# Layer 2's attention of the first batch moved to the end of layer 1, its weights split early and kept in DRAM for both batches

## What is computed

```
# layer 1: 16 heads of 128, each token sees the blocks of 64 within two of its own
x = layernorm(x + softmax(q k^T / sqrt(128) + band_mask) v @ Wo)
# layer 2: a router scores each token; the 128 best of each batch are processed
scores = x @ w_router ;  idx = sort(top_k(scores, 128))
sel = x[b, idx]                       # 256 tokens in all
h = rms_norm(sel) ;  q, k, v = h @ wq + bq, h @ wk + bk, h @ wv + bv
q, k = rope(q, idx), rope(k, idx)     # 16 query heads, 8 key/value heads
x1 = sel + causal_softmax(q k^T / sqrt(128)) v @ wo    # over the 256 tokens
y  = x1 + silu(rms_norm(x1) @ w_gate) * (rms_norm(x1) @ w_up) @ w_down
x[b, idx] = sigmoid(scores) * y + (1 - sigmoid(scores)) * sel ;  x = layernorm(x)
```

## Time and profile before

| | us |
|---|---|
| median of 3 runs | 1465.58 (1464.21 to 1465.84) |
| the profiled execution | 1463.87 |
| its span, first to last instruction | 1462.0 |
| PE busy | 1292.3 (88%) |
| DVE, ACT, POOL busy | 947.5, 588.4, 99.2 |
| PE matmuls of layer 1's q, k, v projections and of the units (proj, L835) | 694.3 |

### The profile page before, as it was taken

The page is one execution under the profiler, slowest core; times in us unless marked ns, Lnnn a source line. Parts: engine busy times, 40 slices in busy tenths (PEclk is TensorE's granted clock), DMA queues, the critical chain, the costliest instruction groups (busy, mean ns, idle before and its releaser), DMA issues.

```text
span 1462.0 us, 20054 instructions
## 1 busy us (share of the span) xinstructions
PE 1292.3 (88%) x7624; PEld 1138.4 (78%) x7624; DVE 947.5 (65%) x2523; ACT 588.4 (40%) x1478; POOL 99.2 (7%) x139
## 2 busy tenths in 40 slices
PE   6999999999999999999998998999999995266696
PEld 5888888888888888787777887788887884265595
DVE  4556566666666666887866676666767667656464
ACT  4444444444444444334434444444444431023341
POOL 0000000000000000110000000000000001112272
PEclk9999999999999999999999999999999998598798
DMA  5000110101010120132112143353434236195251
GB/s 180 30 15 30 44 44 15 44 15 44 15 44 22 52 73 30 63 112 72 44 33 72 67 144 125 138 177 123 170 129 144 98 121 232 55 393 190 86 187 43
DMA packets 75967, 135.76 MB, mean 93 GB/s; under 512 B 4384, under 2 KB 51488, under 8 KB 69728
## 3 DMA queue, kind: packets, MB, share of 16 engines
q1 hardware_dynamic: 75456, 133.19, 26.5%
...
## 4 chain that ended last, share of the span: by engine, by line
PE 39%; DVE 36%; ACT 13%; DMA 6%; issue 4%; POOL 1%; SPq 0%; ACTq 0%; DVEq 0%; POOLq 0%
PE proj L835 21%; DVE arena L1272 14%; ACT prob L1128 6%; ACT arena L1094 5%; PE s L835 5%; PE y L835 5%; PE o L835 4%; DVE prob L1307 4%; DVE arena L1323 4%; DMA w_dram<-arena 3%; DVE yacc L1341 3%; PE tp L907 2%; DMA work<-bqkv 2%; DVE prob L1316 2%; DVE work L1389 2%
## 5 line engine op out<-in xcount | busy, mean ns | idle before, releaser
L835 PE MATMUL proj<-arena 128*128 128x256 f32 (+1 forms) x3804 | 694.3, 333 | 17.4 <-DVE arena L1272 17.0
L835 PEld LDWEIGHTS proj<-arena 128*128 128x128 f32 x3804 | 582.1, 193 | 85.5 <-DVE arena L1272 28.0
L1128 ACT ACTIVATE prob<-prob,stat 128x384 f32<-128x384 f32 (+1 forms) x256 | 151.1, 590 | 541.3 <-DVE stat L1307 541.3
L1272 DVE TENSOR_TENSOR arena<-proj,arena 128x512 fp32r<-128x512 f32 (+2 forms) x282 | 155.7, 559 | 280.9 <-ACT arena L1094 280.7
L835 PE MATMUL s<-arena 128*128 128x384 f32 (+2 forms) x960 | 216.9, 342 | 51.5 <-DVE arena L1272 46.3
L835 PE MATMUL o<-arena 128*128 128x256 f32 (+3 forms) x1008 | 213.0, 332 | 16.0 <-DVE arena L1272 16.0
L835 PEld LDWEIGHTS s<-arena 128*128 128x128 f32 x960 | 165.5, 191 | 78.6 <-DVE arena L1272 58.0
L835 PE MATMUL y<-arena 128*128 128x512 f32 (+2 forms) x924 | 221.4, 377 | 0.5 <-DVE arena L1272 0.5
L835 PEld LDWEIGHTS y<-arena 128*128 128x128 f32 x924 | 161.2, 192 | 26.5 <-DVE arena L1272 2.3
L1323 DVE TENSOR_TENSOR arena<-tp,arena 128x256 fp32r<-128x256 f32 (+2 forms) x346 | 138.4, 422 | 65.3 <-ACT arena L1140 64.3
L1094 ACT ACTIVATE arena<-proj 128x512 fp32r<-128x512 f32 (+2 forms) x282 | 132.7, 482 | 78.0 <-PE proj L835 55.3
...
## 6 DMA issues: line engine op xcount, KB each, us to landing
...
```

The costliest lines, as they stand in the source:

```text
L835: ins = e.matmul(out_ap, l[a], r[b], start=first and i == 0 and j == 0, stop=final and i == n - 1 and j == 2, skip_group_check=skip)
L1128: e.activation(prob[s][:, 0:n], prob[s][:, 0:n], ACT.Exp, bias=stat[:, 4 * s + 1:4 * s + 2], scale=-1.0, accum_out=stat[:, 4 * s + 2:4 * s ...
L1272: e.tensor_tensor(dst_lo, src, dst_hi.bitcast(F32), ALU.subtract).then_inc(*V_.inc(*name, "lo"))
```

## The change

- The 24 pieces of layer 2's attention (now keepA, keepB, keepC) are split in groups 1 to 7 and 11, three in each (`KEEP_IN`), stored in DRAM one step after their split, and their slot is free again at that moment. Both batches' units bring their pieces back from DRAM: 48 `wback` instead of 24.
- In all of layer 1 after the first two pieces the low part of a weight split is made on POOL and not on DVE (`lo_engine`).
- The units of batch 0 start at steps END - 12, END - 6 and END - 2 to END + 3. `choose(1)` starts at step END + 4, and its compares stand in two halves, the first of which needs only the first four tiles.
- The last `out` of layer 1 comes two tiles in a step instead of one.
- Keys and values of batch 0 stay in SBUF: no `ukeep`, no `ukback`. For that the slots beside the five of layer 1 become three instead of five, eight in all instead of ten.
- Rope's multiplication by the cosine goes from POOL to DVE, the division `un` and the row of layer 1's layernorm from DVE to ACT (behind one more small POOL operation, `shift`). `u6` of batch 0 adds up in its bank.

```diff
         slot_at = ([start["w"] + 2 * s * PIECE for s in range(SPLIT_SLOTS)]
-                   + [start["xT"] + 2 * s * PIECE for s in range(2 * XT_N // (2 * PIECE))]
-                   + [start["pT"] + 2 * 512])
+                   + [start["xT"] + 2 * s * PIECE for s in range(3)])
...
-UNIT_GROUPS = range(NG + 3, NG + 7)
+KEEP_IN = {1: 0, 2: 1, 3: 2, 4: 3, 5: 4, 6: 5, 7: 6, 11: 7}
+
+UNIT_STEPS = [END - 12, END - 6] + [END - 2 + n for n in range(6)]
...
-        def unit_pieces(n):
-            return (("uA", 0, n), columns(wq, n)), (("uB", 0, n), columns(wkv, n)), (("uC", 0, n), rows(wo, n))
+        def to_keep(n):
+            return [(("keepA", n), columns(wq, n)), (("keepB", n), columns(wkv, n)), (("keepC", n), rows(wo, n))]
+
+        def come_back(b, n):
+            return [((which, b, n), None) for which in ("uA", "uB", "uC")]
 
         stream = []
         for G in range(NB * NG):
             b, g = divmod(G, NG)
             pieces = dict(q=Wq, v=Wv, k=Wk)
-            stream += [((which, b, g), columns(pieces[which], g)) for which in ("qv" if G > 0 else "qkv")]
-            if G - 1 in UNIT_GROUPS:
-                stream.append(unit_pieces(2 * UNIT_GROUPS.index(G - 1))[2])
-            if G > 0:
-                stream.append((("k", b, g), columns(Wk, g)))
-            if G - 1 in UNIT_GROUPS:
-                stream += unit_pieces(2 * UNIT_GROUPS.index(G - 1) + 1)[:2]
+            kept = to_keep(KEEP_IN[G]) if G in KEEP_IN else []
+            stream += [((which, b, g), columns(pieces[which], g)) for which in ("qvk" if G > 0 else "qkv")]
+            stream += kept[:1]
             if G >= 1:
                 stream.append((("o", *divmod(G - 1, NG)), rows(Wo, (G - 1) % NG)))
-            if G - 1 in UNIT_GROUPS:
-                stream.append(unit_pieces(2 * UNIT_GROUPS.index(G - 1) + 1)[2])
-            if G in UNIT_GROUPS:
-                stream += unit_pieces(2 * UNIT_GROUPS.index(G))[:2]
+            stream += kept[1:]
+        stream += come_back(0, 0) + come_back(0, 1)[:2]
...
         stream.append((("o", NB - 1, NG - 1), rows(Wo, NG - 1)))
-        for n in range(NKV):
-            stream += [((which, 1, n), None) for which in ("uA", "uB", "uC")]
+        stream += come_back(0, 1)[2:]
+        for b in range(NB):
+            for n in range(2 if b == 0 else 0, NKV):
+                stream += come_back(b, n)
...
                 job("wsave", n)
+                free_slots.append((slot_of[n], None, n))
...
             for half in range(2):
-                while not (tail or bank1_free[0]):
+                while (b, 4 * half + 3) not in normed or not (tail or bank1_free[0]):
                     yield
                 take(half, ("rows", b, half), S_, "rows", b, half, "copy")
-                hold(f"work{3 + half}", ("rows", b, half), V_, "tied", b, "rank")
+                hold(rows_in[half], ("rows", b, half), V_, "rank", b, "rank")
                 job("rows", b, half)
-            yield
-            for a in range(TT):
-                if a == 0:
-                    hold("work2", ("count", b, 0), V_, "tied", b, "rank")
-                    hold("work5", ("count", b, 0), V_, "tied", b, "rank")
-                job("count", b, a)
-                if not tail or a % 4 == 3:
-                    yield
+                yield
+                for i, what in enumerate(COMPARES[half]):
+                    if half == 0 and i < 2:
+                        hold(junk_in[i], ("count", b, i), V_, "rank", b, "rank")
+                    job(what[0], b, *what[1:])
+                    if not tail and i % 2:
+                        yield
             job("rank", b)
-            for a in range(TT):
-                job("tie", b, a)
-                if not tail and a % 2:
-                    yield
-            job("tied", b)
+            load_ln("work3" if tail else "work4", b, V_, "rinh", b, "h")
...
+        lo_engine[0] = lambda n: "G"
...
-            if 0 <= u - END < TT:
-                project_out(NB * NG - 1, u - END)
-                running.append(finish_layer1(NB - 1, u - END))
+            for t in range(TT):
+                if u - END == t // 2 + (t >= TT // 2):
+                    project_out(NB * NG - 1, t)
+                    running.append(finish_layer1(NB - 1, t))
             if u - 16 * NG in NORM_STEPS:
                 running.append(finish_layer1(0, NORM_STEPS.index(u - 16 * NG)))
             if u == NG * HG * TT + 23:
                 running.append(choose(0))
-            if G in UNIT_GROUPS and r in (4, 12):
-                n = 2 * UNIT_GROUPS.index(G) + (r == 12)
-                here, there = ("proj1", "y") if r == 4 else ("y", "proj1")
-                running.append(unit(0, n, [here] * 4 + [there] * 2))
+            if u == END + 4:
+                running.append(choose(1))
+            if u in UNIT_STEPS:
+                n = UNIT_STEPS.index(u)
+                of = f"proj{1 - n % 2}"
+                running.append(unit(0, n, [of] * 5 + ["y"] if n < 2 else [of, "tp", "o0", "tp", "o1", "y"]))
...
-            if u == END + 3:
-                add_slots([PT_SLOT], "pv", NHEADS - 1, TT - 1, "made")
...
+                elif kind == "lnorm":
+                    b, t = key
+                    i, row = t % 2, yacc[:, t, :]
+                    act.wait_ge(*G_.at("ln", b, t, "shift"))
+                    e.activation(row, row, ACT.Identity, bias=shift[i][:], scale=rstd[i][:]).then_inc(*S_.inc("lnorm", b, t, "row"))
+
...
+                elif kind == "un":
+                    b, n = key
+                    nk = (b + 1) * P
+                    mine, rc = uprob[b, n % 2], stat[:, 20 + 8 * (n % 2):22 + 8 * (n % 2)]
+                    act.wait_ge(*V_.at("un", b, n, "recip"))
+                    for h in range(2):
+                        ins = e.activation(mine[:, h * nk:(h + 1) * nk], mine[:, h * nk:(h + 1) * nk], ACT.Copy,
+                                           scale=rc[:, h:h + 1])
+                    ins.then_inc(*S_.inc("un", b, n, "prob"))
...
                     after(e.tensor_tensor(by_sin[:, :, H2:HD], heads[:, :, 0:H2], over_heads(sinf[:, H2:HD], H2), ALU.mult),
                           "ur", b, n, "sin1")
-                    dve.wait_ge(*G_.at("u1", b, n, "cos"))
-                    e.tensor_tensor(work[m][:, 0:3 * HD], work[a][:, 0:3 * HD], work[m][:, 0:3 * HD], ALU.add
+                    after(e.tensor_tensor(heads, heads, over_heads(rope_sel[:, 0:HD], HD), ALU.mult), "ur", b, n, "cos")
+                    e.tensor_tensor(work[m][:, 0:3 * HD], work[bs][:, 0:3 * HD], work[m][:, 0:3 * HD], ALU.add
...
-                    dve.wait_ge(*G_.at("ln", b, t, "rstd"))
-                    after(e.tensor_scalar(row, row, mv[i][:, 0:1], rstd[i][:], ALU.subtract, ALU.mult),
-                          "lnorm", b, t, "row")
+                    dve.wait_ge(*S_.at("lnorm", b, t, "row"))
+                    dve.wait_ge(*freed("products", "lnorm", b, t))
...
+                    if kind == "ln":
+                        pool.wait_ge(*G_.at(kind, b, t, "rstd"))
+                        e.tensor_scalar(shift[i][:], mv[i][:, 0:1], rstd[i][:], -1.0, ALU.mult, ALU.mult
+                                        ).then_inc(*G_.inc(kind, b, t, "shift"))
```

326 lines of the change are left out of this document (143 added, 183 removed).

## The result

The changed kernel takes 1478.76 us (median of 4 runs, 1475.2 to 1479.54), against 1464.89 for the kernel before on the same chips: a ratio of 1.0093, 95% interval 1.0071 to 1.0116. It is slower by 14 us; 1483.0 was forecast. The profiled execution took 1478.81, its span 1477.1.

The account below looks back on a forecast made before the run. It took PE (TensorE, 88% busy) to bound layer 1, with another limit behind it. 1463.9 - 76.6 + 12 + 62 - 7 + 26 + 1 = 1481.3, plus 1.7 for the median: 1483.0 us; 8 in 10 range 1428 to 1508.

Parts of the forecast that it names:

- Term 1: Groups 11 to 14 of layer 1: batch 0's eight units leave with their splits and stores, -76.6 us.
- Term 2: Last twelve steps of layer 1: units 0 and 1 run there, +12 us, bounds 0 and 19.
- Term 3: Eight groups with kept pieces: ACT waits for stores through one slot, +62 us, the main term; bounds +8 and +112.
- the slack of 1.0: Groups with kept pieces: ACT's slack, taken as 1.0 us off the 7.4 us a chain of stores is late.
- the 1.3 for clock and division: Groups with kept pieces: 1.3 us added per group for PE's falling clock and DVE's division beside POOL.
- Term 4: Groups 7 to 10: DVE relieved of low parts and layernorm rows, -7 us, bounds -14 and +5; plain groups nothing.
- Term 5: Behind layer 1: the choice for batch 1 comes later, +26 us, bounds +6 and +40.
- first compare 21 later: Behind layer 1: batch 1's first compare at 53 us, 21 later than before, with 5 us for late pieces.
- Term 6: Batch 1's units: eight slots instead of ten, +1 us, bounds -5 and +8.
- Rival A: Groups with kept pieces: stores land in time, their cost is 8 us and the time 1429; chance 0.22.
- rival B: Behind layer 1: the choice is hardly later, +6 us, time 1463; chance 0.14.
- rival C: All of layer 1: POOL and DVE hinder each other, 34 us, time 1517; chance 0.10.

Follow-up runs that it names:

- experiment 5: Changed kernel with each kept piece's store issued ahead of the next split's load and its slot given free two steps later: 1427.1 us, ratio 0.9748.
- experiment 11: Changed kernel with experiment 5's edit, experiment 7's edit, and units 2 to 7 of batch 0 started two steps earlier: 1427.44 us, ratio 0.9743.
- experiment 2: Changed kernel with the low parts of layer 1's weight splits back on DVE instead of POOL: 1471.54 us, ratio 1.0078.
- experiment 6: Experiment 5's kernel with layer 1's low parts on DVE instead of POOL: 1449.48 us, ratio 0.9904.
- experiment 10: Experiment 5's kernel with layer 1's layernorm row back on DVE instead of ACT: 1429.83 us, ratio 0.9765.
- experiment 8: Changed kernel with only the high half of each of batch 0's 24 pieces brought back from DRAM, 12 MB less: 1468.64 us, ratio 1.0057.
- experiment 7: Changed kernel with batch 1's prefix sums, position search and gather directly behind the compares, no unit stage between: 1475.01 us, ratio 1.0094.

## Why the forecast held, point by point

**Term 1, units out of groups 11 to 14: -76.6 forecast, -71.8 measured.** Groups 12 to 14 are at 66.9, 67.0 and 66.3. Group 11 is at 74.2; experiments 5 and 11 have 72.6 and 74.2 there, so its excess is not the store waits, and was not looked into.

**Term 2, two units at the end of layer 1: +12 forecast, +9.6 measured.**

**Term 3, stores of kept pieces: +62 forecast, +54 measured** by undoing it alone (experiment 5: group 15 begins at 1075.7 and not 1129.9). The mechanism is the one predicted, and so is its length: links of 12.5 and twice 9.9 us, 32.4 in all, where it had 12.5 and twice 10.1, 32.7. A chain is so 7.1 us late against its six steps, where 7.4 was forecast. What was paid is 6.9 a group (73.8 against 66.9): neither the slack of 1.0 nor the 1.3 for clock and division shows as such, and they nearly cancelled in the sum.

Two readings around it were off. The prediction expected waits of 4, 2 and 2 in a group; they are 4.0 each. And it took from the earlier trace rows that an ACT wait is paid about one for one; 94.9 us of ACT waiting cost 54. The reason that fits is that an ACT wait also holds time in which ACT would have had nothing to do, and the chain's lateness does not. Experiment 2 says the same: three waits of 1.7 on average a group, a chain that is 3.3 late (28.6 us), and 2.4 paid (70.7 against experiment 6's 68.3). The gap of 4.56 us in PE behind a wait of 3.35 was the largest of seven; the others are 1.9 to 3.5, and each is longer than its wait, so such a gap holds more than the wait and is not its price.

**Term 4, DVE relieved: -7 forecast, with -14 as its bound; about -24 measured.** With no store waits in the way, groups 7 to 10 take 291.7 us against 306.0 (-14.3), and the rest comes where the prediction had zero: up to group 1 (108.4 against 114.5) and in groups 1 to 6 (66.9 against 67.4, together -3.4). The step that failed is "in plain groups DVE has 17 us of 50 free, so its relief is worth nothing". It holds nearly for plain groups as they were, with four low parts: 0.3 and 0.5 us in groups 12 and 13, and -0.6 in 14 (experiment 6 against the changed kernel). But groups 1 to 6 were no longer plain. The change splits three more pieces in each, and there POOL is worth 1.4 us a group, and 10.0 up to group 1. A reason that fits is that a low part on DVE stands ahead of a short operation on whose end PE waits, whatever DVE's mean load is; no run shows it. And of the 14.3 only 5.8 come from the low parts (experiment 6) and none from the row (experiment 10). The other 8.5 lie in groups 9 and 10: with low parts on DVE as before, these two take 69.8 and 71.5 us in experiment 6 and 73.1 and 80.5 in the kernel before, and group 8 takes 3 more. That is where the choice for batch 0 runs, which is now cut into other pieces, but also where the kernel before already splits pieces of its first units. Neither was tried by itself.

**Term 5, the choice comes later: +26 forecast, with +40 as its bound; +47 measured.** The largest miss. Its step "first compare 21 later" gave 30.8 (it counted from a tile 2.5 us ahead of the last, which makes its 53 about 51 by the table's count). It had 5 us for late pieces, and PE's waits for pieces there are 6.8; what it had at nothing are the 7.6 us that DVE waits for the bias rows `bqkv`, queued behind pieces. Experiment 8 takes away all of these and half of the others, and the first compare comes 11 earlier. Its step "units between the compares and the prefix sums cost 5 more" gave 16: 3.7 in the compares, 9.2 between chosen tokens and positions, 3.4 behind. The 9.2 are two unit stages. A tiny product of the choice runs on PE, and the product of a unit's output, 2.91 us at a granted clock of 0.50, stands directly behind it, at 1260.29 and at 1267.25. DVE's next small step for the choice stands behind DVE's part of that stage, which waits for ACT and so for PE:

```profile
1271.11 0.42 DVE L1289 TENSOR_TENSOR arena<-o,arena 128x256 fp32r<-128x256 f32 x1 [4.16 <-ACT arena L1096]
```

So the choice passes from 1267.01 on PE to 1271.86 on DVE, the positions. With no stage between them the positions come 2.8 us behind the chosen tokens (experiment 7). The prediction spoke of DVE and of the first rows of scores, and did not price what stands between the last steps, where nothing of the choice can run ahead.

**Term 6: +1 forecast, -0.4 measured.**

So the forecast came to within 5 us with terms 3 and 4 too dear by 8 and 17 and term 5 too cheap by 21. The main term was right by its mechanism; that the sum was this close is luck, since errors of 25 and 21 us cancelled. Rival A (stores land in time) is excluded by the shortest landing of 5.7; rival B (choice hardly later) by 104.4 us against 57.3; rival C (POOL and DVE hinder each other at the price of 34 us) by experiment 6. They do hinder each other, and by it DVE's division takes 520 ns on average in the changed kernel where it took 404:

```profile
L1333 DVE TENSOR_SCALAR prob<-prob,stat 128x384 f32<-128x384 f32 (+1 forms) x256 | 133.2, 520 | 9.1
```

The Trainium skill, "SBUF — State Buffer", section Who interferes with whom, draws the line here: a tensor_scalar can enter a two-port mode and then contends with GpSimd, whoever issues first shutting the other out, and an instruction with one input from SBUF outside these modes does not. The traces agree, 404 to 488 or 520 ns against 561 and 561. What the rule could not tell is the balance: 21 to 30 us of stretched divisions against 103 us of low parts taken over.

That the change is slower is no fault of its idea. Taking the units out of layer 1 is worth 62 us net (terms 1 and 2), and the low parts on POOL with the rest of term 4 are worth 24. The later choice costs 47, and 54 were lost in one slot that was used again too soon.
